# Post-norm transformer block on one core: projections of blocks 3 and 4 moved ahead of and into step 0, roots, doubling and sign activations reordered in the first four steps

## The chip, the cores and the metric
The kernel runs on one core of a Trainium2 chip. The metric is the device time of one execution in microseconds (us); the time of a kernel is the median of its runs.

## The reference
One layer on x of 4096 tokens by 256 channels: sliding-window attention with 16 heads of 16 channels, then a two-layer network with binarised weights, each with a residual and a layer norm behind it.

```python
q = _l2norm(proj(Wq)); k = _l2norm(proj(Wk)); v = proj(Wv)
attn = einsum('bhqd,bhkd->bhqk', q, k)
mask = (rel < 0) | (rel >= 128)              # rel = key position - query position
attn = softmax(attn + where(mask, -1e30, -|rel| * slope_h))
x = layernorm(x + einsum(attn, v) @ Wo.T)
h = gelu(x @ (alpha1 * sign(w1)).T + b1)     # alpha = mean |w| of a row
x = layernorm(x + h @ (alpha2 * sign(w2)).T + b2)
```

## The kernel before
The 4096 tokens are 32 blocks of 128. Each engine has its program written out by hand; the engines meet at semaphores, and each runs its own instructions strictly in the written order. Blocks are projected three steps ahead of their use, so "step i" handles different blocks at a time:

- TensorE (`step` in the tensor program): scores of block i in four chunks of four heads (L342), the query and key projection of block i+3 in two halves between them (`project_qk`, L368), values of block i+1 (`project_v`, L379), the turns of the strips and rows of block i-2 and the output projection (L387, L394, L402), and four chunks of weighted sums (L357). A chunk of scores uses one of two pairs of banks, so chunk 2 waits for the exponential of chunk 0.
- ScalarE: the copy of the weighted sums into strips (L593), four exponentials (`exps`, L616), the copy oT (L599), squares of block i+3 (L569), its root as logarithm and exponential (`norm_of`, L574, L576), and the high halves of block i+2 in float16 (`high_halves`, L583, L586).
- VectorE: `double` of block i+1 (L813, a float16 copy), `outputs` (reciprocal L786, otok L789), the faded values vdiag and vnext (L837, L839), layer norm statistics, the sums of squares and the seed of block i+3 (L859, L769), three operations of a Newton round (`rsqrt_round`, L774, L776, L778), and the normalised block qkn (L876).
- GpSimd: the triangular cuts of each chunk of probabilities (L1162), then the low halves of block i+2 (`low_halves`, L1173, L1175). `double` waits for these.
- SP (the DMA queue): loads of blocks (L243, L244), weights, and `turn_parts` (L256), which transposes the doubled halves into qkT. The scores of a block wait for its transpose. The transpose of block n waits for `double(n)`.

Around the loops stand some extras: dummy matmuls (`keep_warm`, WARM_AGAIN of them ahead of step 0), sign activations of w2 and w1 (`signs2`, `signs1`, L641, L645), and sums of |w2| in halves (`abs_w2`, L908). Steps -3 to -1 prepare blocks 0 to 2; steps 0 to 3 are written out, steps 4 and on are loops. Step 0 has neither queries of a next block nor weighted sums, so it uses chunks of 128x512 instead of 128x1024. After step 31 come eight groups of the two-layer network.

Names of semaphores that the words below use: qkn_done counts normalised blocks, exp_done exponentials, lo_done low halves, parts_ready doubled blocks, otok_done and onorm_done the turned and the scaled outputs, sgn_ready the sign activations.

Of the kernel before, what the change touches and what calls it, by code (L numbers as in the profile page):

```python
# [11 lines left out]
ALU = mybir.AluOpType  # L12
# [3 lines left out]
P = 128  # L16
D = 256
DC = D // P
# [26 lines left out]

WARM_AGAIN = 14

# [54 lines left out]
def norm_base(i, next3):  # L102

    return (i + 3) * NORM_OPS if next3 else NB * NORM_OPS + (i - NB + 3) * (NORM_OPS - 1) - 1
# [7 lines left out]
def build(nc, x, xT, wqkvT, woT, w1, w1T, b1c, w2T, b2, out):  # L112
    with ExitStack() as ctx:
# [215 lines left out]
        def _(pe):  # L329
# [43 lines left out]
            def project_v(i, slot, prev3):  # L373

                count(pe, v_ready, i + 1)
                if prev3:
                    pe.wait_ge(resid_done, i - 2)
                for k in range(DC):
                    mm = nc.tensor.matmul(ps[:, VO, 0:D], xt[:, slot, k, :], wqkv[:, k, 2 * D:3 * D],  # L379
                                          start=(k == 0), stop=(k == DC - 1))  # L380
                mm.then_inc(v_done, 1)
# [63 lines left out]
            pe.wait_ge(wv_in, 16)  # L445
            project_v(-1, 0, False)
            keep_warm(WARM_AGAIN)
            pe.wait_ge(id_made, 2)
            pe.wait_ge(consts, 2)
            step(0, 0, 0, pv=False, prev2=False, prev3=False, both=False)  # L450
            step(1, 1, 1, prev2=False, prev3=False)
            pe.wait_ge(wo_in, 16)
# [45 lines left out]
            def first_hidden():  # L498

                pe.wait_ge(sgn_ready, 2)  # L500
                pe.wait_ge(prep, 1)
                hidden(0, 0, 0)
# [61 lines left out]
        def _(act):  # L564
# [36 lines left out]

            def step(i, par, prev2=True, next2=True, next3=True, prev3=True, early2=False, both=True):
                if prev2:
# [16 lines left out]
                if early2:  # L620
                    high_halves(i, par)
                if prev2:
                    take_rows(i)
                exps(2)
                if next3:
                    squares(i, par)
                exps(3)
                if next3 or prev3:
                    norm_of(i, next3, prev3)
# [8 lines left out]

            def signs2():
                act.wait_ge(w2_in, 16)  # L640
                nc.scalar.activation(sgn2[:], w2_t[:], ACT.Sign).then_inc(sgn_ready, 1)  # L641

            def signs1():
                act.wait_ge(mlp_in, 16 * 3)
                nc.scalar.activation(sgn1[:], w1_t[:], ACT.Sign).then_inc(sgn_ready, 1)  # L645

# [10 lines left out]
            norm_of(-1, True, False)  # L657
            signs2()
            step(0, 0, prev2=False, prev3=False, early2=True, both=False)
            step(1, 1, prev2=False, prev3=False)  # L660
            signs1()
            step(2, 0, prev3=False)
            step(3, 1)
            with act.Fori(0, (NB - 12) // 2) as t:
# [101 lines left out]
        def _(dve):  # L766
# [49 lines left out]
            def split_keys(n):  # L816
# [6 lines left out]
                double(n, n)  # L823

            def step(i, par, cur=True, prev2=True, next1=True, next3=True, prev3=True, prev4=True, aside=None, amid=None):
                base, cols = norm_base(i, next3), norm_columns(next3, prev3)
                norm = (half[:, cols], nt_a[:, cols], nt_b[:, cols], rnorm[:, cols], newton, base)
                if next1:
# [26 lines left out]
                if next3:  # L855

                    dve.wait_ge(sq_done, i + 4)
                    count(dve, newton, base - NORM_OPS + 1)
                    nc.vector.tensor_reduce(ss[:], sq[:].rearrange("p (h d) -> p h d", d=HD), AX.X,  # L859
                                            ALU.add).then_inc(ss_done, 1)  # L860
                    dve.wait_ge(ss_done, i + 4)
                    count(dve, qkn_done, i + 3)
                    if prev3:
                        dve.wait_ge(ln_seed, i - 2)
                    rsqrt_seed(ss[:], half[:, 0:2 * H], (NORM_EPS / QK_SCALE) ** 2, ALU.max, newton)
                if prev2:
# [3 lines left out]
                if next3 or prev3:  # L870
                    rsqrt_round(*norm)
                if next3:

                    dve.wait_ge(newton, base + NORM_OPS)
                    count(dve, lo_done, i + 2)
                    nc.vector.tensor_tensor(qkn[:, 1 - par, :].rearrange("p (h d) -> p h d", d=HD),  # L876
                                            ps[:, QK[1 - par], :].rearrange("p (h d) -> p h d", d=HD),
                                            rnorm[:, 0:2 * H].unsqueeze(2).to_broadcast([P, 2 * H, HD]),
                                            ALU.mult).then_inc(qkn_done, 1)
            nc.vector.memset(mean_ones[:], 1.0 / HID).then_inc(layout, 1)  # L880
# [46 lines left out]
            dve.wait_ge(first_low, 2)  # L927
            step(0, 0, prev2=False, next1=False, prev3=False, prev4=False, aside=lambda: abs_w2(0))
            step(1, 1, prev2=False, prev3=False, prev4=False)
            step(2, 0, prev3=False, prev4=False, aside=lambda: abs_w2(1))  # L930
# [358 lines left out]
```

## Time and profile before
| | us |
|---|---|
| median of 3 runs | 399.65 |
| lowest, highest | 398.71, 401.49 |
| profiled execution, its own time | 399.07 |
| its span, first to last instruction | 397.3 |
| busy TensorE / VectorE / ScalarE / GpSimd | 370.4 / 312.2 / 310.9 / 274.9 |
| mean granted TensorE clock | 0.993 |

The span leaves out 1.8 us of the execution. Busy shares are means over stages with different limits: 30 us of start, attention steps until about 280 us, the network after it. All times below count from the start of the span.

### The profile page before, as it was taken

To read this page: it belongs to the slowest core of one execution; us is meant where nothing else is said; L and a number is where in the kernel's file an instruction comes from. 1 tells how busy PE (TensorE), PEld (TensorE's weight loads), DVE (VectorE), ACT (ScalarE), POOL (GpSimd) and SP (SyncE) were. 2 spreads that over 40 slices of the span, in tenths; PEclk is the share of its full clock that TensorE was granted. 3 is DMA by queue.
4 is the path that set the end of the run, shared out by engine and by line. 5 is a ranking of instruction groups with operands and counts; after the bars stand their busy time and mean duration, and the time that the engine had idled before them with its cause. 6 is when DMAs were issued, how large, how long until landed. Compare 5 with 4: busy or idle time off the path is not lost. (4 is left out here: it accounts for less than half of the span.)

```text
span 397.3 us, 12038 instructions
## 1 busy us (share of the span) xinstructions
PE 370.4 (93%) x3921; PEld 234.9 (59%) x3921; DVE 312.2 (79%) x856; ACT 310.9 (78%) x532; POOL 274.9 (69%) x418
## 2 busy tenths in 40 slices
PE   7788999999999999999999899899999999999991
PEld 5545566655665666556655556555566666666671
DVE  3968777787777777877778878656889998999985
ACT  3688788788877887888788778778988888887744
POOL 1287888888888888888888789888236645655221
PEclk9999999999999999999999999999999999999997
DMA  6694577446434543464345446440022215303112
GB/s 220 143 282 85 120 121 182 86 89 123 106 79 89 121 107 79 88 122 107 79 88 113 94 105 90 89 93 2 1 54 54 79 29 107 106 0 106 55 53 106
DMA packets 98542, 38.28 MB, mean 96 GB/s; under 512 B 84688, under 2 KB 97360, under 8 KB 98256
## 3 DMA queue, kind: packets, MB, share of 16 engines
q1 hardware_dynamic: 98512, 37.89, 43.1%
q8 instruction: 17, 0.28, 0.3%
q14 instruction: 13, 0.11, 0.1%
HBM read 12.72 MB, written 4.19 MB: 43 GB/s over the span
## 5 line engine op out<-in xcount | busy, mean ns | idle before, releaser
L1162 POOL TENSOR_SCALAR_AFFINE_SELECT prob<-prob 128x512 f32<-128x512 f32 x252 | 154.1, 642 | 35.3 <-ACT prob L616 35.3
L616 ACT ACTIVATE prob<-ps 128x1024 f32<-128x1024 f32 (+1 forms) x128 | 125.7, 1014 | 0.7 <-PE ps L342 0.7
L368 PE MATMUL ps<-wqkv,xt 128*128 128x512 f32 x128 | 66.2, 605 | 2.2 <-DVE qkn L876 1.9
L520 PE MATMUL ps<-sgn,prob 128*128 128x256 f16 x512 | 61.5, 273 | 1.5 <-DVE prob L985 1.5
L494 PE MATMUL ps<-yT,sgn 128*128 128x512 f16 x256 | 61.2, 379 | 1.1 <-issue 0.6
L678 ACT ACTIVATE ps<-ps,bias,alpha 128x512 f32<-128x512 f32 x64 | 47.7, 750 | 15.7 <-PE ps L494 12.4
L520 PEld LDWEIGHTS ps<-sgn,prob 128*128 128x128 f16 x512 | 50.0, 98 | 14.8 <-DVE prob L985 2.9
L1221 POOL TENSOR_TENSOR resid<-z,resid 128x256 f32 (+1 forms) x31 | 22.5, 726 | 50.2 <-DVE z L995 50.2
L357 PE MATMUL ps<-prob,vdiag 128*17 128x128 f32 x1024 | 51.2, 274 | 1.7 <-POOL prob L1162 1.6
L342 PEld LDWEIGHTS ps<-qkT 64*128 64x128 f16 x512 | 17.2, 94 | 56.4 <-issue 31.4
L357 PE MATMUL ps<-prob,vnext 128*17 128x128 f32 x992 | 49.7, 273 | 0.0
L342 PE MATMUL ps<-qkT 64*128 64x256 f16 (+1 forms) x512 | 44.2, 272 | 3.2 <-DMA qkT<-parts 2.3
L985 DVE SCALAR_TENSOR_TENSOR prob<-ps,h_scale,prob 128x512 f16<-128x512 f32 x64 | 45.1, 743 | 0.4 <-ACT prob L684 0.3
L593 ACT ACTIVATE strips<-ps 128x512 f32<-128x512 f32 x32 | 19.1, 596 | 27.2 <-PE ps L357 27.2
L859 DVE TENSOR_REDUCE ss<-sq 128x32 f32<-128x512 f32 x32 | 22.0, 686 | 23.1 <-ACT sq L569 22.9
L494 PEld LDWEIGHTS ps<-yT,sgn 128*128 128x128 f16 x256 | 24.6, 98 | 24.4 <-issue 1.0
L684 ACT ACTIVATE prob<-ps,h_scale 128x512 f16<-128x512 f32 x61 | 38.6, 683 | 0.1
L379 PE MATMUL ps<-wqkv,xt 128*128 128x256 f32 x128 | 36.1, 405 | 0.0
L1175 POOL TENSOR_TENSOR parts<-qkn,parts 128x512 f16<-128x512 f32 x30 | 34.8, 1159 | 0.0
L357 PEld LDWEIGHTS ps<-prob,vdiag 128*17 128x17 f32 x1024 | 25.4, 97 | 13.7 <-issue 10.4
L402 PE MATMUL ps<-wo,oT 128*128 128x256 f32 x128 | 33.0, 380 | 0.1
L357 PEld LDWEIGHTS ps<-prob,vnext 128*17 128x17 f32 x992 | 28.1, 98 | 0.0
(105 smaller groups left out, 577.2 us busy)
## 6 DMA issues: line engine op xcount, KB each, us to landing
xt<-in_xT SPq DMA_DIRECT2D x32, 128.0 KB, 2.8
resid<-in_x SPq DMA_DIRECT2D x32, 128.0 KB, 2.3
out_dram<-resid SPq DMA_DIRECT2D x7, 512.0 KB, 2.9
w_t<-in_w2T SPq DMA_DIRECT2D x1, 1024.0 KB, 7.8
w_t<-in_w1T SPq DMA_DIRECT2D x1, 1024.0 KB, 5.0
w_nat<-in_w SPq DMA_DIRECT2D x4, 256.0 KB, 4.2
wqkv<-in_wqkvT SPq DMA_DIRECT2D x3, 256.0 KB, 4.1
qkT<-parts SPq DMA_TRANSPOSE x32, 4.3
```

Of the source, the lines that this page charges most:

```text
L342: mm = nc.tensor.matmul(ps[:, SC + 2 * (c % 2) + hp, 2 * P * t:2 * P * t + wide], qkT[row, here, H // 2 + 2 * c + t, :], queries, start=Tr ...
L357: mm = nc.tensor.matmul(ps[32 * m:32 * m + HD + 1, OT, P * c:P * c + P], v, prob[:, s, CH * c + m, P * (1 - par):P * (1 - par) + P], start ...
L368: mm = nc.tensor.matmul(ps[:, QK[1 - par], :], xt[:, slot, k, :], wqkv[:, k, 0:2 * D], start=(k == 0), stop=(k == DC - 1))
L379: mm = nc.tensor.matmul(ps[:, VO, 0:D], xt[:, slot, k, :], wqkv[:, k, 2 * D:3 * D], start=(k == 0), stop=(k == DC - 1))
L494: mm = nc.tensor.matmul(ps[:, bank, :], sgn1[:, c, P * k:P * k + P], yT[:, par, a, c, :, :], start=(m == 0), stop=(m == 2 * DC - 1))
L520: mm = nc.tensor.matmul(ps[:, banks[b], 0:D], hid[:, par, a, k, P * b:P * b + P], sgn2[:, k, :], start=(m == 0), stop=(m == 2 * HC - 1))
L616: nc.scalar.activation(to, scored, ACT.Exp, scale=QK_SCALE ** -2).then_inc(exp_done, 1)
L678: nc.scalar.activation(bank, bank, ACT.Gelu, bias=bias1[:, k:k + 1], scale=alpha1[:, k:k + 1]).then_inc(gelu_done, 1)
L684: nc.scalar.activation(hid[:, par, 0, k, :], ps[:, hidden_bank(n, k, par), :], ACT.Copy, scale=h_scale[:]).then_inc(hhi_done, 1)
L985: nc.vector.scalar_tensor_tensor(out=hid[:, par, 1, k, :], in0=bank, scalar=h_scale[:], in1=hid[:, par, 0, k, :], op0=ALU.mult, op1=ALU.su ...
L1162: sel = nc.gpsimd.affine_select(out=at, in_=at, compare_op=ALU.is_ge, fill=0.0, base=-near, pattern=[[0, CH], [1 if near else -1, P]], cha ...
L1175: nc.gpsimd.tensor_tensor(parts[:, par, H:2 * H, 2:4, :], src[:, H:2 * H, :].unsqueeze(2).to_broadcast([P, H, 2, HD]), parts[:, par, H:2 * ...
```

## The change
TensorE: block 3's projection (i = 0) goes ahead of step 0, in front of the dummy matmuls, of which 6 are left from 14; block 4's projection stands whole in step 0, behind its first two chunks of scores. Steps 0 and 1 have no projections between their scores any more. ScalarE: squares of block 3 come before step 0, its root stands behind the second exponential of step 0, block 4's squares behind the fourth, and block 4's root behind the second exponential of step 1. The sign activations are in halves: w2's first half ahead of step 0, its second behind step 1, and w1's halves behind the fourth exponentials of steps 2 and 3. VectorE: sums of block 3 ahead of `abs_w2(0)`, its round and normalisation behind it, then `double(2)` and the sums of block 4, all ahead of step 1's values. The later wait for sgn_ready counts 4 instead of 2. GpSimd and SP keep their order.

```diff
-WARM_AGAIN = 14
+WARM_AGAIN = 6
...
             project_v(-1, 0, False)
+            for k in range(DC):
+                project_qk(0, 0, 3, k)
             keep_warm(WARM_AGAIN)
...
+            def project_fourth():
+                for k in range(DC):
+                    project_qk(1, 1, 0, k)
-            step(0, 0, 0, pv=False, prev2=False, prev3=False, both=False)
-            step(1, 1, 1, prev2=False, prev3=False)
+            step(0, 0, 0, pv=False, prev2=False, prev3=False, next3=False, both=False, between=project_fourth)
+            step(1, 1, 1, prev2=False, prev3=False, next3=False)
...
                 exps(1)
                 if early2:
                     high_halves(i, par)
+                if amid:
+                    amid()
...
                 exps(3)
+                if aside:
+                    aside()
...
-            signs2()
-            step(0, 0, prev2=False, prev3=False, early2=True, both=False)
-            step(1, 1, prev2=False, prev3=False)
-            signs1()
-            step(2, 0, prev3=False)
-            step(3, 1)
+            squares(0, 0)
+            signs2(0)
+            step(0, 0, prev2=False, next3=False, prev3=False, early2=True, both=False, amid=lambda: norm_of(0, True, False),
+                 aside=lambda: squares(1, 1))
+            step(1, 1, prev2=False, next3=False, prev3=False, amid=lambda: norm_of(1, True, False))
+            signs2(1)
+            step(2, 0, prev3=False, aside=lambda: signs1(0))
+            step(3, 1, aside=lambda: signs1(1))
...
-            step(0, 0, prev2=False, next1=False, prev3=False, prev4=False, aside=lambda: abs_w2(0))
-            step(1, 1, prev2=False, prev3=False, prev4=False)
+            step(0, 0, prev2=False, next1=False, next3=False, prev3=False, prev4=False)
+            norm_sums(0, False)
+            abs_w2(0)
+            rsqrt_round(*norm_tiles(0, True, False))
+            normalise_rows(0, 0)
+            double(2, 0)
+            norm_sums(1, False)
+            step(1, 1, prev2=False, next1=False, next3=False, prev3=False, prev4=False)
+            rsqrt_round(*norm_tiles(1, True, False))
+            normalise_rows(1, 1)
```

`norm_sums`, `norm_tiles` and `normalise_rows` are the parts of VectorE's step that were written inside it: the sum of squares with the seed, the tiles of the round, and the normalised block.

ScalarE in steps 0 and 1 before: sq are squares, lnx and rnorm the root, prob the exponentials (128x4x128 in step 0), parts the high halves.

```order
L616 ACTIVATE prob<-ps 128x4x128
L569 ACTIVATE sq<-ps 128x512
L616 ACTIVATE prob<-ps 128x4x128
L574 ACTIVATE lnx<-half 128x32
L576 ACTIVATE rnorm<-lnx 128x32
L616 ACTIVATE prob<-ps 128x1024 x3
L569 ACTIVATE sq<-ps 128x512
L616 ACTIVATE prob<-ps 128x1024
L574 ACTIVATE lnx<-half 128x32
L576 ACTIVATE rnorm<-lnx 128x32
```

The same stretch after the change.

```order
L582 ACTIVATE lnx<-half 128x32
L584 ACTIVATE rnorm<-lnx 128x32
L624 ACTIVATE prob<-ps 128x4x128 x2
L577 ACTIVATE sq<-ps 128x512
L624 ACTIVATE prob<-ps 128x1024 x2
L582 ACTIVATE lnx<-half 128x32
L584 ACTIVATE rnorm<-lnx 128x32
L624 ACTIVATE prob<-ps 128x1024 x2
```

Block 3's root has left the place between the steps, and block 4's stands between the second and third exponential of step 1.

VectorE between the values of step 0 and those of step 1 before: w_sum is `abs_w2(0)`, parts the doubling of block 2.

```order
L908 TENSOR_REDUCE w_sum<-w_t 128x128
L859 TENSOR_REDUCE ss<-sq 128x32
L769 TENSOR_SCALAR half<-ss 128x32
L774 TENSOR_TENSOR nt_a<-half,rnorm 128x32
L776 TENSOR_TENSOR nt_b<-nt_a,rnorm 128x32
L778 SCALAR_TENSOR_TENSOR rnorm<-nt_b,rnorm 128x32
L876 TENSOR_TENSOR qkn<-ps,rnorm 128x512
L813 COPY parts<-parts 128x16x32
L837 TENSOR_TENSOR vdiag<-ps,fade 128x16x16
```

The same stretch after the change.

```order
L854 TENSOR_REDUCE ss<-sq 128x32
L789 TENSOR_SCALAR half<-ss 128x32
L939 TENSOR_REDUCE w_sum<-w_t 128x128
L794 TENSOR_TENSOR nt_a<-half,rnorm 128x32
L796 TENSOR_TENSOR nt_b<-nt_a,rnorm 128x32
L798 SCALAR_TENSOR_TENSOR rnorm<-nt_b,rnorm 128x32
L866 TENSOR_TENSOR qkn<-ps,rnorm 128x512
L833 COPY parts<-parts 128x16x32
L854 TENSOR_REDUCE ss<-sq 128x32
L789 TENSOR_SCALAR half<-ss 128x32
L882 TENSOR_TENSOR vdiag<-ps,fade 128x16x16
```

The sums of block 3 are ahead of `abs_w2(0)`, and the sums of block 4 ahead of step 1's values.

ScalarE in step 2 after the change, from the third exponential to the high halves (before, the sign row was not there and all 2048 columns stood ahead of step 2's strips).

```order
L624 ACTIVATE prob<-ps 128x1024
L577 ACTIVATE sq<-ps 128x512
L624 ACTIVATE prob<-ps 128x1024
L656 ACTIVATE sgn<-w_t 128x1024
L582 ACTIVATE lnx<-half 128x32
L584 ACTIVATE rnorm<-lnx 128x32
L591 ACTIVATE parts<-qkn 128x16x16
L594 ACTIVATE parts<-qkn 128x16x32
```

A half of the signs has come in ahead of the root.

## Rows read from the trace of the kernel before

**Rows 1.** Timeline of step 3, then step 25's strips: start, duration, engine, line [idle before]
```profile
38.54 0.60 ACT L593 ACTIVATE strips<-ps 128x512 f32<-128x512 f32 x1 [0.94 <-PE ps L357]
...
40.64 0.39 PE L342 MATMUL ps<-qkT 64*128 64x256 f16 x4
...
40.96 0.44 PE L394 MATMUL ps<-id,otok 128*128 128x128 f32 x2
...
213.36 0.60 ACT L593 ACTIVATE strips<-ps 128x512 f32<-128x512 f32 x1 [0.45 <-PE ps L357]
```

**Rows 2.** Timeline from the end of step 1 into step 2
```profile
28.61 1.90 ACT L645 ACTIVATE sgn<-w_t 128x2048 f16<-128x2048 f32 x1
...
29.07 0.41 PE L357 MATMUL ps<-prob,vdiag 128*17 128x128 f32 x8 [0.54 <-POOL prob L1162]
...
30.41 0.58 ACT L593 ACTIVATE strips<-ps 128x512 f32<-128x512 f32 x1
...
30.73 0.61 PE L342 MATMUL ps<-qkT 64*128 64x256 f16 x8 [1.03 <-DMA qkT<-parts]
...
31.17 1.94 ACT L616 ACTIVATE prob<-ps 128x1024 f32<-128x1024 f32 x2 [0.18 <-PE ps L342]
```

**Rows 3.** Timeline from the projections through steps 0 and 1
```profile
10.98 1.96 PE L368 MATMUL ps<-wqkv,xt 128*128 128x512 f32 x4 [1.92 <-DVE qkn L876]
...
13.46 0.69 DVE L876 TENSOR_TENSOR qkn<-ps,rnorm 128x512 f32<-128x512 f32 x1
...
15.79 0.43 SPq L244 DMA_DIRECT2D resid<-in_x  x1
...
18.04 1.94 DVE L908 TENSOR_REDUCE w_sum<-w_t 128x128 f32<-128x1024 f32 x1
...
20.89 1.15 POOL L1175 TENSOR_TENSOR parts<-qkn,parts 128x512 f16<-128x512 f32 x1
...
21.28 0.69 DVE L859 TENSOR_REDUCE ss<-sq 128x32 f32<-128x512 f32 x1 [1.30 <-ACT sq L569]
...
23.10 2.83 ACT L616 ACTIVATE prob<-ps 128x1024 f32<-128x1024 f32 x3
...
24.51 0.50 DVE L813 COPY parts<-parts 128x512 f16<-128x512 f16 x1
...
27.91 0.57 DVE L774 TENSOR_TENSOR nt_a<-half,rnorm 128x32 f32<-128x32 f32 x1 [0.56 <-ACT rnorm L576]
```

**Rows 4.** DMA issues of 14 to 20 us, then of 24 to 28; last: us to landing
```profile
resid<-in_x SPq DMA_DIRECT2D x1, 128.0 KB, 2.8
...
qkT<-parts SPq DMA_TRANSPOSE x1, 5.4
```

**Rows 5.** Timeline from step 2 into step 3
```profile
36.99 0.61 ACT L586 ACTIVATE parts<-qkn 128x512 f16<-128x512 f32 x1
...
38.38 1.16 POOL L1175 TENSOR_TENSOR parts<-qkn,parts 128x512 f16<-128x512 f32 x1
...
39.61 0.28 DVE L813 COPY parts<-parts 128x512 f16<-128x512 f16 x1
...
40.19 2.40 POOL L1162 TENSOR_SCALAR_AFFINE_SELECT prob<-prob 128x512 f32<-128x512 f32 x4 [0.65 <-ACT prob L616]
```

**Rows 6.** Timeline of a late step, around its doubling
```profile
214.52 0.67 POOL L1203 TENSOR_TENSOR yparts<-resid,yparts 128x256 f16<-128x256 f32 x1
214.59 0.75 DVE L813 COPY parts<-parts 128x512 f16<-128x512 f16 x1 [0.96 <-POOL parts L1175]
...
216.02 0.44 PE L394 MATMUL ps<-id,otok 128*128 128x128 f32 x2 [0.18 <-DVE otok L789]
```

**Rows 7.** Stretches: busy us of PE, PEld, DVE, ACT, POOL; PEclk; DMA share, GB/s
```profile
27.00:30.00 3.00, 2.16 (x64) 1.41 (x64) 2.31 (x6) 2.92 (x6) 3.00 (x6) 1.00 1.24 156
...
388.00:391.90 3.90, 0.96 (x9) 0.61 (x7) 3.32 (x15) 2.71 (x8) 1.34 (x2) 1.00 0.36 129
391.90:397.30 5.40, 0.00 (x0) 0.00 (x0) 1.73 (x8) 1.28 (x4) 0.00 (x0) 0.50 0.29 101
```

More of the change, by code:

```diff
@@ L498, in first_hidden @@
             def first_hidden():
-                pe.wait_ge(sgn_ready, 2)
+                pe.wait_ge(sgn_ready, 4)
                 pe.wait_ge(prep, 1)
@@ L600, in take_rows, with step @@
                                      ACT.Copy).then_inc(ot_ready, 1)
-            def step(i, par, prev2=True, next2=True, next3=True, prev3=True, early2=False, both=True):
+            def step(i, par, prev2=True, next2=True, next3=True, prev3=True, early2=False, both=True, amid=None, aside=None):
                 if prev2:
@@ L637, in norm_of, with signs, signs2, signs1 @@
                 root(half[:, cols], lnx[:, cols], rnorm[:, cols], newton, base, 1)
[L639 to L645, printed above, removed]
+            def signs(dst, src, loaded, times, part):
+                half_ = slice(part * HID, part * HID + HID)
+                flat = "p k n -> p (k n)"
+                act.wait_ge(loaded, 16 * times)
+                nc.scalar.activation(dst[:].rearrange(flat)[:, half_], src[:].rearrange(flat)[:, half_],
+                                     ACT.Sign).then_inc(sgn_ready, 1)
+            def signs2(part):
+                signs(sgn2, w2_t, w2_in, 1, part)
+            def signs1(part):
+                signs(sgn1, w1_t, mlp_in, 3, part)
             nc.scalar.preload_act_table_set("natural_log_exp_and_others")
@@ L823, in split_keys, with norm_tiles, norm_sums, normalise_rows @@
                 double(n, n)
+            def norm_tiles(i, next3, prev3):
+                cols = norm_columns(next3, prev3)
+                return half[:, cols], nt_a[:, cols], nt_b[:, cols], rnorm[:, cols], newton, norm_base(i, next3)
+            def norm_sums(i, prev3):
+                dve.wait_ge(sq_done, i + 4)
+                count(dve, newton, norm_base(i, True) - NORM_OPS + 1)
+                nc.vector.tensor_reduce(ss[:], sq[:].rearrange("p (h d) -> p h d", d=HD), AX.X,
+                                        ALU.add).then_inc(ss_done, 1)
+                dve.wait_ge(ss_done, i + 4)
+                count(dve, qkn_done, i + 3)
+                if prev3:
+                    dve.wait_ge(ln_seed, i - 2)
+                rsqrt_seed(ss[:], half[:, 0:2 * H], (NORM_EPS / QK_SCALE) ** 2, ALU.max, newton)
+            def normalise_rows(i, par):
+                dve.wait_ge(newton, norm_base(i, True) + NORM_OPS)
+                count(dve, lo_done, i + 2)
+                nc.vector.tensor_tensor(qkn[:, 1 - par, :].rearrange("p (h d) -> p h d", d=HD),
+                                        ps[:, QK[1 - par], :].rearrange("p (h d) -> p h d", d=HD),
+                                        rnorm[:, 0:2 * H].unsqueeze(2).to_broadcast([P, 2 * H, HD]),
+                                        ALU.mult).then_inc(qkn_done, 1)
             def step(i, par, cur=True, prev2=True, next1=True, next3=True, prev3=True, prev4=True, aside=None, amid=None):
-                base, cols = norm_base(i, next3), norm_columns(next3, prev3)
-                norm = (half[:, cols], nt_a[:, cols], nt_b[:, cols], rnorm[:, cols], newton, base)
+                base = norm_base(i, next3)
                 if next1:
@@ L855, in step @@
                 if next3:
[L857 to L865, printed above, removed]
+                    norm_sums(i, prev3)
                 if prev2:
@@ L870, in step @@
                 if next3 or prev3:
-                    rsqrt_round(*norm)
+                    rsqrt_round(*norm_tiles(i, next3, prev3))
                 if next3:
[L874 to L879, printed above, removed]
+                    normalise_rows(i, par)
             nc.vector.memset(mean_ones[:], 1.0 / HID).then_inc(layout, 1)
```

## Prediction

> **What bounds the kernel now.** The kernel is a pipeline of 32 attention steps, and I read first what one step hands to the next. ScalarE's strip copy (L593) starts at 38.54 in step 3 and at 213.36 us, 22 steps later [rows 1]: a period of 7.95 us. In one period the chain is: strips, exponential of chunk 0, then TensorE's third scores at 40.64, the turn of the rows at 40.96, and from there TensorE without a gap until the last weighted sum, which releases the next strips [rows 1]. There is no slack in that chain after the strips. So whatever delays or advances the strips and first exponential of step 2 is kept for the rest of the run, and so is every stall put into one step. The change touches only steps -1 to 3, so its worth is one sum of such shifts.
>
> The entry into step 2 is where the timeline shows gaps [rows 2]: the last weighted sum of step 1 starts at 29.07, when GpSimd's last cut allows it; the strips start at 30.41, held by the whole sign activation of 1.90 us at 28.61; the scores of step 2 start at 30.73, when the transposed block 2 has landed, and its first exponential at 31.17. The transpose was issued when block 2 had been doubled, at 25.0 [rows 3], and landed 5.4 us later [rows 4]. Three things are nearly level there: the transpose (30.5), ScalarE's signs (30.4), and GpSimd's cuts (29.0), behind which the last sums run for some 0.65 us.
>
> **Steps 0 and 1 after the change**, in the clock of this trace.
> TensorE: block 3's projection fits where the dummy matmuls were. It needs the second normalised block (L876, 13.46 + 0.69), takes 1.96 us like the projection at 10.98 [rows 3], and is over at 16.2; six dummies follow. The scores of step 0 wait for the same transpose as before. Then `project_fourth` waits for block 4, whose second load is issued at 15.79 and lands 2.8 us later, 18.6 [rows 3, 4]. With 1.96 us for it the third scores come at 20.6, the first scores of step 1 at 22.1 and ScalarE's first wide exponential, 0.44 later as in step 2 [rows 2], at 22.5. Before it was 23.10 [rows 3]. So far the change wins 0.6 us, since ScalarE no longer waits for block 3's root between the steps.
>
> VectorE: block 3's sums (0.69 us and a seed of 0.2) go ahead of abs_w2, which starts about 18.95 instead of 18.04 and takes 1.94 us [rows 3]. The root's round then starts at 20.9. That is the bad moment: GpSimd's long subtraction L1175 starts at 20.89 and runs 1.15 us to 22.04 [rows 3], then come two cuts of 0.6 (four take 2.4 [rows 5]). The trace shows that a small VectorE operation beside a busy GpSimd lasts until GpSimd's current instruction ends: nt_a at 27.91 takes 0.57 us, the copy of double at 24.51 takes 0.50 against 0.28 at 39.61 [rows 3, 5]. So the three operations of the round end at about 22.1, 22.7 and 23.3 instead of taking 0.65 in all; the normalised block 3 is there at 24.0 and block 2 is doubled at 24.4, against 25.0 now. Uncontended it would be 22.8. I take the contended value, as the rows overlap by position, and keep 22.8 for the range.
>
> The Trainium skill, SBUF — State Buffer, "SBUF: two separate sides", says that VectorE and GpSimd share a port pair under an exclusive lock, held for the whole instruction, for VectorE operations with two SBUF inputs or in a two-port mode. Its rule gives the same 24.4, whereas a view in which the engines only share bandwidth would give 22.8; the rows just named side with the lock.
>
> Block 4's sums follow: 0.69 us, and the seed is caught by a cut again, so half is ready at 25.5. ScalarE now has the root of block 4 between its second and third exponential; the second ends at 22.5 + 1.94 = 24.45, so ScalarE waits about 1.05 us for VectorE and starts the third exponential only at 25.95. Two exponentials end at 27.9. The 0.6 won is lost here. GpSimd's last two cuts (1.2 us) start at 28.3 and end at 29.5 instead of 29.0; the last sums start at 29.55, 0.48 later than in [rows 2]. ScalarE's splitting of block 3 and half a sign end at 29.6, the strips start at 30.25 when the sums end, and the first exponential of step 2 at 30.75. The transpose, issued at 24.5, lands by 29.9 if it takes 5.4 again: not last any more.
> Entry: 31.17 - 30.75 = **0.4 us won**. Bounds: with the uncontended value ScalarE does not wait, cuts end at 28.45, the strips come at 29.15 and the exponential at 29.65, 1.5 us won (if the transpose lands in under 5.4); if the transpose still lands at 30.5, 0.2 us won.
>
> **Signs in halves.** Before, all of w1's signs stood in the gap of [rows 2]. Half of them (1024 columns) takes between 0.95, half of 1.90, and 1.04, a 1024-column exponential; I take 1.03. One half now stands in step 2 and one in step 3, between the fourth exponential and the root. ScalarE has 0.94 us idle ahead of the strips at 38.54 [rows 1], so the strips there are hardly later. But the root and the split of the block (L583, L586 until 37.60 [rows 5]) move back by 0.8 us, to 38.4. GpSimd's low halves follow: L1175, now 38.38 to 39.54, ends at 40.3. Now there is a free stretch on GpSimd until the first cut at 40.19 in which VectorE doubles at 39.61 [rows 5]. It is gone: the first cut starts as L1175 ends, and the double, which waits for L1175, meets a busy GpSimd. That case is in the trace: at 214.52 a GpSimd subtraction starts right behind L1175, the double at 214.59 takes 0.75 us, and the turn of the rows starts at 216.02, released by otok, 0.68 us after the double's end [rows 6]. Here the double would run 40.35 to 41.1 and the turn of the rows start at 41.8 instead of 40.96: **0.8 us lost in step 3**. Behind the double are the reciprocal and otok, and TensorE and ScalarE's oT wait for them. Were the double to get in first (0.28 us), the loss is 0.4. The same in step 4 from the second half: 0.8, or 0.4.
>
> **No cost:** eight dummy matmuls fewer, hidden in the wait for block 0's transpose. The half sign ahead of step 0 ends at 17.8, before the first scores are done. SP's order is unchanged; the transpose of block 3 goes out at about 31.7, behind GpSimd's low halves, and has landed by 37.1 even at 5.4 us, ahead of the scores that come just before the strips at 38.54.
>
> **Sum:** -0.4 + 0.8 + 0.8 = **+1.2 us**. The profiled execution took 399.07 us (span 397.3 and 1.8 around it), so 400.3 on its scale; on the median of the three runs, 399.65, it is 400.85. I put the forecast between, at 400.6.
>
> **Rivals.**
> A, the port is free at block 3's root: the entry wins 1.5, stalls cost 1.6: +0.1 us, 399.2 to 399.8. For it: a few tenths in when L1175 runs decide. Against: abs_w2 ends within 0.1 us of its start.
> B, the signs cost nothing: ScalarE's idle 0.94 covers them and the turn of the rows, which could start at 40.57 (39.61 + 0.28 + 0.68 [rows 5, 6]) and starts at 40.96, hides 0.4 more. Then only the entry counts: -0.4 to -1.5, 398.1 to 399.3. Against it are [rows 5, 6].
> C, the early doubling gives nothing, since block 2's transpose is behind w1 and six blocks of loads in the DMA queues; it lands at 30.5 and the entry wins 0.2: +1.4, or 400.8; with more wait at block 4's root up to +2, 401.6.
> D, clearly slower: TensorE's clock falls. The granted clock is 1.00 (2.4 GHz) in all of step 1 with TensorE busy 2.16 of 3 us; at the end of the run it is 0.50 (1.2 GHz) from 391.9, after TensorE had been busy 0.96 of 3.9 us [rows 7]. Fewer dummies and waits in step 1 make TensorE idler. It decides if an idle stretch comes near the 2.9 us that it had before 391.9; I work out 1.5 us at most. One step at the lower clock would add up to the 5.7 us from the third scores to the next strips: 405 us or more.
> The Trainium skill, TensorE: Matmul & The Clock Gate, "What's actually happening", says the throttled state is the default and activity releases it; by that rule D is possible.
>
> **Chances.** Forecast 0.45, A 0.2, B 0.17, C 0.15, D 0.03. A measurement of this kernel tells about 1% (4 us) from no change; the three runs alone span 2.8 us. All but D lie within 1%: same 0.95, faster 0.02 (B with more won on the transpose than I can find), slower 0.03. The range takes the bounds -1.5 to +2 around the two scales: 398.2 to 401.9 us.
>
> **What would show it.** In the profile after: the first wide exponential near 22.5, a gap of about 1 us on ScalarE before block 4's root, nt_a of block 3 over 1 us, double of block 2 near 24.4, its transpose landing before 30, the strips of step 2 near 30.25; double in steps 3 and 4 at 0.75 us and TensorE waiting for otok there; periods of 8.7 us twice, 7.95 after. Strips at 38.1 and 46.1 would mean B. Wrong altogether would be another period than 7.95 in the loop.

## The result and the profile after

The changed kernel takes 401.87 us (median of 20 runs, 400.92 to 403.52) against 400.03 us before (20 runs beside it, 398.71 to 402.11): ratio 1.004, 95% interval 1.0028 to 1.0052, that is 1.1 to 2.1 us slower. The forecast was 1.2 us slower and 400.6 us, inside a range of 398.2 to 401.9. The profiled execution took 401.66 us, its span 399.6. All ratios below leave aside one execution of the experiment e6, which took 613.41 us at a mean granted clock of 0.56.

The timeline of the changed kernel from step 0 to the strips of step 2 (start, duration, engine, line, operation, [idle before <- releaser]):

```profile
18.92 1.98 PE L368 MATMUL ps<-wqkv,xt 128*128 128x512 f32 x4 [0.31 <-DMA resid<-in_x]
...
21.21 1.16 POOL L1214 TENSOR_TENSOR parts<-qkn,parts 128x512 f16<-128x512 f32 x1
...
21.71 0.70 DVE L794 TENSOR_TENSOR nt_a<-half,rnorm 128x32 f32<-128x32 f32 x1
...
22.33 1.22 POOL L1201 TENSOR_SCALAR_AFFINE_SELECT prob<-prob 128x512 f32<-128x512 f32 x2
22.45 0.55 DVE L796 TENSOR_TENSOR nt_b<-nt_a,rnorm 128x32 f32<-128x32 f32 x1
22.66 1.94 ACT L624 ACTIVATE prob<-ps 128x1024 f32<-128x1024 f32 x2
23.04 0.55 DVE L798 SCALAR_TENSOR_TENSOR rnorm<-nt_b,rnorm 128x32 f32<-128x32 f32 x1
...
24.23 0.36 DVE L833 COPY parts<-parts 128x512 f16<-128x512 f16 x1
...
25.73 0.23 ACT L582 ACTIVATE lnx<-half 128x32 f32<-128x32 f32 x1 [1.14 <-DVE half L789]
...
29.71 0.41 PE L357 MATMUL ps<-prob,vdiag 128*17 128x128 f32 x8 [0.54 <-POOL prob L1201]
...
30.41 0.60 ACT L601 ACTIVATE strips<-ps 128x512 f32<-128x512 f32 x1 [0.59 <-PE ps L357]
31.38 0.61 PE L342 MATMUL ps<-qkT 64*128 64x256 f16 x8 [1.03 <-DMA qkT<-parts]
...
31.81 1.94 ACT L624 ACTIVATE prob<-ps 128x1024 f32<-128x1024 f32 x2 [0.80 <-PE ps L342]
```

It follows the working of the prediction closely up to the strips. The first wide exponential is at 22.66 (23.10 in [rows 3]), the three operations of block 3's round take 0.70, 0.55 and 0.55 us beside GpSimd, ScalarE waits 1.14 us for block 4's half, the last sums start 0.64 us later than in [rows 2], and the strips at 30.41. Then comes a row that the forecast did not have: the scores of step 2 wait for the transpose of block 2 until 31.38, and ScalarE waits 0.80 us behind them. The first exponential of step 2 is 0.64 us later than in [rows 2] instead of 0.4 earlier.

Half of that 0.64 us was there before step 0 began. In this execution the granted clock was 0.50 from 11.1 to 14.5 us; the projection in that stretch took 3.37 us instead of the 1.96 of [rows 3], and TensorE came to the first scores of step 0 after their transpose had landed:

```profile
10.71 3.37 PE L368 MATMUL ps<-wqkv,xt 128*128 128x512 f32 x4 [1.92 <-DVE qkn L866]
...
18.21 0.40 PE L342 MATMUL ps<-qkT 64*128 64x128 f16 x8
...
18.53 1.08 ACT L624 ACTIVATE prob<-ps 128x512 f32<-128x512 f32 x2
```

In the kernel before they waited for it:

```profile
17.88 0.40 PE L342 MATMUL ps<-qkT 64*128 64x128 f16 x8 [0.96 <-DMA qkT<-parts]
...
18.21 1.08 ACT L616 ACTIVATE prob<-ps 128x512 f32<-128x512 f32 x2 [0.50 <-PE ps L342]
```

So the first exponential of step 0 was 0.32 us late already. Counted from it, the first exponential of step 2 comes after 12.96 us before and 13.28 us after: the entry itself lost 0.32 us.

The transpose had been issued at 24.66, earlier than before. The DMA issues between 24 and 28 us, with the us to landing last, against the 5.4 of [rows 4]:

```profile
qkT<-parts SPq DMA_TRANSPOSE x1, 6.5
```

Step 3 of the changed kernel, in the same timeline form, around the doubling of block 4:

```profile
39.18 0.60 ACT L601 ACTIVATE strips<-ps 128x512 f32<-128x512 f32 x1 [0.16 <-PE ps L357]
...
39.79 1.22 POOL L1214 TENSOR_TENSOR parts<-qkn,parts 128x512 f16<-128x512 f32 x1
...
40.97 2.44 POOL L1201 TENSOR_SCALAR_AFFINE_SELECT prob<-prob 128x512 f32<-128x512 f32 x4
41.04 0.70 DVE L833 COPY parts<-parts 128x512 f16<-128x512 f16 x1 [1.05 <-POOL parts L1214]
...
42.42 0.44 PE L394 MATMUL ps<-id,otok 128*128 128x128 f32 x2 [0.75 <-DVE otok L809]
...
42.90 0.38 ACT L607 ACTIVATE oT<-ps 128x256 f32<-128x256 f32 x1 [1.29 <-PE ps L394]
...
47.99 0.60 ACT L601 ACTIVATE strips<-ps 128x512 f32<-128x512 f32 x1 [0.24 <-PE ps L357]
...
49.72 0.70 DVE L833 COPY parts<-parts 128x512 f16<-128x512 f16 x1 [1.38 <-POOL parts L1214]
```

GpSimd goes from L1214 straight into the cuts at 40.97, the doubling starts 0.07 us later and takes 0.70 instead of the 0.28 of [rows 5], and TensorE waits for otok. The period of step 3, strips to strips, is 8.81 us, where the kernel before has 7.99; that of step 4 is 8.60 against 7.91. From there on both kernels alternate between 7.99 and 7.91, so the three shifts, 0.64 + 0.82 + 0.69 = 2.15 us, are carried to the end of attention: the last strips start at 279.29 instead of 277.19. The spans differ by 2.3 us. Without the 0.32 us from ahead of step 0 the shifts are 1.83 us, and the medians differ by 1.84.

### The profile page after: what moved, and what is told of

The parts are those of the page before. It is cut to its first block and busy times, and to the rows that moved or that the text cites. A ratio compares the mean times of both kernels' runs of the same rounds, so it can differ in the third digit from the quotient of the medians.

```text
span 399.6 us, 12008 instructions
## 1 busy us (share of the span) xinstructions
PE 369.4 (92%) x3905; PEld 233.3 (58%) x3905; DVE 309.7 (77%) x856; ACT 310.7 (78%) x534; POOL 275.0 (69%) x418
## 5 line engine op out<-in xcount | busy, mean ns | idle before, releaser
L1201 POOL TENSOR_SCALAR_AFFINE_SELECT prob<-prob 128x512 f32<-128x512 f32 x252 | 154.3, 643 | 35.3 <-ACT prob L624 35.3
L1260 POOL TENSOR_TENSOR resid<-z,resid 128x256 f32 (+1 forms) x31 | 22.5, 725 | 50.4 <-DVE z L1034 50.4
L502 PEld LDWEIGHTS ps<-yT,sgn 128*128 128x128 f16 x256 | 24.6, 98 | 24.5 <-issue 1.1
L1214 POOL TENSOR_TENSOR parts<-qkn,parts 128x512 f16<-128x512 f32 x30 | 34.9, 1162 | 0.0
L357 PEld LDWEIGHTS ps<-prob,vdiag 128*17 128x17 f32 x1024 | 25.4, 97 | 13.7 <-issue 10.4
L379 PEld LDWEIGHTS ps<-wqkv,xt 128*128 128x128 f32 x128 | 22.1, 192 | 10.6 <-issue 7.2
```

The costliest lines, as they stand in the source:

```text
L357: mm = nc.tensor.matmul(ps[32 * m:32 * m + HD + 1, OT, P * c:P * c + P], v, prob[:, s, CH * c + m, P * (1 - par):P * (1 - par) + P], start ...
L502: mm = nc.tensor.matmul(ps[:, bank, :], sgn1[:, c, P * k:P * k + P], yT[:, par, a, c, :, :], start=(m == 0), stop=(m == 2 * DC - 1))
L1201: sel = nc.gpsimd.affine_select(out=at, in_=at, compare_op=ALU.is_ge, fill=0.0, base=-near, pattern=[[0, CH], [1 if near else -1, P]], cha ...
```

## The experiments

Each experiment was timed in five rounds against the kernel before on the same chip: e1 to e4 together, e5 to e8 together, e9 to e11 together. They have 11 or 12 executions each, e4 has 6. "Landing" is read from the sixteen semaphore increments of the transpose: the last one, and the last but one in brackets. "Packet" is the start of the first 16 KB packet, after the loads at the start, on queue q8, which the profile names "instruction". "Start" is the first exponential of step 0.

| kernel | ratio to before (95%) | start | packet | issue, landing of block 2's transpose | step 2's first exponential |
|---|---|---|---|---|---|
| before | | 18.21 | 25.4 | 25.08, 30.49 (30.48) | 31.17 |
| changed | 1.0040 (1.0028 to 1.0052) | 18.53 | 29.1 | 24.66, 31.13 (29.65) | 31.81 |
| e1 | 1.0016 (0.9993 to 1.0039) | 17.65 | 28.3 | 23.52, 30.32 (28.84) | 31.00 |
| e2 | 1.0024 (1.0011 to 1.0037) | 18.72 | 29.2 | 24.66, 31.26 (29.78) | 32.03 |
| e3 | 0.9976 (0.9962 to 0.9990) | 18.32 | 28.4 | 24.44, 28.98 (28.76) | 30.69 |
| e4 | 1.0063 (1.0039 to 1.0087) | 18.20 | 26.0 | 25.07, 31.13 (31.11) | 31.81 |
| e5 | 1.0012 (0.9993 to 1.0031) | 18.48 | 29.5 | 25.35, 31.52 (30.02) | 32.42 |
| e6 | 0.9978 (0.9964 to 0.9992) | 18.77 | 24.3 | 25.75, 30.01 (29.98) | 30.68 |
| e7 | 0.9985 (0.9971 to 0.9999) | 18.70 | 28.0 | 24.17, 30.13 (28.63) | 32.12 |
| e8 | 1.0045 (1.0026 to 1.0063) | 18.82 | 29.4 | 24.46, 31.43 (29.92) | 32.41 |
| e9 | 0.9972 (0.9961 to 0.9983) | 18.55 | 23.8 | 24.02, 28.47 (28.41) | 30.45 |
| e10 | 1.0006 (0.9990 to 1.0022) | 17.71 | 25.0 | 24.60, 30.12 (30.10) | 30.80 |
| e11 (e3 again) | 0.9964 (0.9948 to 0.9980) | 18.11 | 28.2 | 23.59, 30.16 (28.58) | 30.84 |

The times of the profiles are of one execution each, and the start alone lies anywhere from 17.65 to 18.82 us, in kernels of both kinds, so times of step 2 are to be compared by their distance from it; the ratios are what the verdicts rest on.

### e1: w1's signs ahead of step 2 again
```diff
-            step(2, 0, prev3=False, aside=lambda: signs1(0))
-            step(3, 1, aside=lambda: signs1(1))
+            signs1(0)
+            signs1(1)
+            step(2, 0, prev3=False)
+            step(3, 1)
```


> The changed kernel with both halves of w1's signs back to back ahead of step 2's strips, as the kernel before had them whole. Theory 1 (the halves inside steps 2 and 3 push the doubling into a busy GpSimd): the doublings of blocks 4 and 5 take 0.28 to 0.30 us again, the periods after step 2 are 8.0 and 7.9, and 1.6 us come back; but w2's second half and w1's signs now stand one behind another at the end of step 1, so step 2's strips start near 31.9 and its first exponential near 32.4, 0.6 later than in the changed kernel: about 0.9 us faster than the changed kernel, some 0.7 us slower than the kernel before. Rival (the loss is all in the entry to step 2, halves cost nothing): periods unchanged at 8.8 and 8.6, and 0.6 us slower than the changed kernel.

Measured: doublings of blocks 4 and 5 in 0.28 and 0.30 us, periods of steps 3 and 4 of 7.99 and 7.91, and a ratio of 1.0016, so by the two ratios about 1 us of the loss is gone, as expected, though the two intervals overlap. The rival, unchanged periods, is out. The strips of step 2 came at 30.20, not 31.9: three half signs in a row took 2.94 us from 27.36 and were mostly covered by the wait for the transpose, which again was the last to arrive (scores at 30.57).

### e2: the halves behind the high halves
```diff
-            step(2, 0, prev3=False, aside=lambda: signs1(0))
-            step(3, 1, aside=lambda: signs1(1))
+            step(2, 0, prev3=False)
+            signs1(0)
+            step(3, 1)
+            signs1(1)
```


> The changed kernel with each half of w1's signs behind the high halves of steps 2 and 3 instead of ahead of the root. ScalarE does the same work in the same steps; only the order against the root and the split differs. Theory 1: GpSimd's low halves are on time, doublings of blocks 4 and 5 at 0.28 to 0.30 us, strips of steps 3 and 4 about 0.15 us late (a half of 1.05 to 1.08 us against 0.94 us of idle time), so periods of 8.1 us instead of 8.8 and 8.6: 1.3 us faster than the changed kernel, 0.3 to 0.6 us slower than the kernel before. Rival (halves cost ScalarE time alone): no difference to the changed kernel.

The timeline of e2 in step 3:

```profile
38.38 1.04 ACT L656 ACTIVATE sgn<-w_t 128x1024 f16<-128x1024 f32 x1
39.26 1.16 POOL L1216 TENSOR_TENSOR parts<-qkn,parts 128x512 f16<-128x512 f32 x1
39.41 0.60 ACT L601 ACTIVATE strips<-ps 128x512 f32<-128x512 f32 x1
...
40.49 0.28 DVE L835 COPY parts<-parts 128x512 f16<-128x512 f16 x1
41.05 2.40 POOL L1203 TENSOR_SCALAR_AFFINE_SELECT prob<-prob 128x512 f32<-128x512 f32 x4 [0.64 <-ACT prob L624]
...
41.83 0.44 PE L394 MATMUL ps<-id,otok 128*128 128x128 f32 x2
```

GpSimd is idle again for 0.64 us ahead of the cuts, the doubling fits in, and TensorE does not wait for otok. ScalarE does the same work as in the changed kernel, in the same steps. The periods of steps 3 and 4 are 7.99 and 7.91. So a half sign there is free, and the place ahead of the root alone cost the 0.7 to 0.8 us of each step. Its ratio is 0.16% below the changed kernel's, 0.6 us, with intervals that overlap; the medians differ by 1.8 us (400.09 and 401.87), but were not timed together. The times that settle it are those of e4 and e10 below.

### e4: the same edit alone, on the kernel before
```diff
-            signs1()
-            step(2, 0, prev3=False)
-            step(3, 1)
+            step(2, 0, prev3=False, aside=lambda: signs1(0))
+            step(3, 1, aside=lambda: signs1(1))
```


> The kernel before with one edit: w1's signs in halves behind the fourth exponentials of steps 2 and 3, as the change has them. Theory 1: doublings of blocks 4 and 5 at 0.70 to 0.75 us, TensorE waits for otok, periods 8.7 to 8.8 and 8.6; the entry does not gain, since the transpose of block 2 lands at 30.5 as before: 1.5 us slower than the kernel before. Rival (the entry is what the change loses, not the halves): within 0.3 us of the kernel before.

Here and in e6 and e10, `signs1(part)` does one half of the columns, as in the change, and the later wait for sgn_ready counts 3.

Measured: 1.9 us slower in the medians (401.36 and 399.44), 1.6 to 3.5 us by the ratio. The doublings took 0.70 us twice and the periods were 8.81 and 8.59, the changed kernel's to 0.01 us. This edit alone gives a loss as large as the change's, and 1.5 us of it are the two stalls. The entry was not level, as expected: the transpose of block 2 took 6.1 us instead of 5.4, and the first exponential of step 2 came at 31.81, 0.64 us late, from an equal start. The edit does not explain that.

### e10: the halves behind the high halves, on the kernel before
```diff
-            signs1()
             step(2, 0, prev3=False)
+            signs1(0)
             step(3, 1)
+            signs1(1)
```


> The kernel before with one edit: w1's signs in halves behind the high halves of steps 2 and 3. Theory (halves cost nothing there and the entry is bound by block 2's transpose): transpose lands at 30.5 and step 2's first exponential stays at 31.2; doublings of blocks 4 and 5 at 0.28 to 0.30 us; within 0.5 us of the kernel before. Rival (the whole signs at the end of step 1 held the entry): first exponential at 30.3 to 30.6, 0.6 us or more faster.

Ratio 1.0006: no difference. Against e4 only the place of the halves differs, four instructions later; that takes the ratio from 1.0063 to 1.0006, and the intervals are apart (1.0039 to 1.0087, 0.9990 to 1.0022). The strips of step 2 came at 29.29, 1.1 us earlier than before (0.6 us counted from the start), and nothing followed from it, as the next rows of its timeline show:

```profile
29.29 0.60 ACT L593 ACTIVATE strips<-ps 128x512 f32<-128x512 f32 x1 [1.07 <-PE ps L357]
...
30.37 0.61 PE L342 MATMUL ps<-qkT 64*128 64x256 f16 x8 [1.15 <-DMA qkT<-parts]
30.80 1.94 ACT L616 ACTIVATE prob<-ps 128x1024 f32<-128x1024 f32 x2 [0.92 <-PE ps L342]
```

In the kernel before, too, the scores of step 2 waited for the transpose [rows 2]; the signs were hidden beneath it.

### e3 and e11: w1's loads behind block 2's transpose
e2, and in SP's program:
```diff
-            for dst, src in ((w1_t, w1T), (bias1, b1c), (bias2, b2)):
-                sp.dma_start(dst[:], src).then_inc(mlp_in, 16)
             for n in range(XS):
                 sp.dma_start(resid[:, n, :], x[n]).then_inc(first_resid, 16)
             load_block(XS + 1, 1)
             turn_parts(2, 2)
+            for dst, src in ((w1_t, w1T), (bias1, b1c), (bias2, b2)):
+                sp.dma_start(dst[:], src).then_inc(mlp_in, 16)
```


> As the run with the halves behind the split, and SP issues the loads of w1, b1 and b2 behind block 2's transpose instead of six loads ahead of it. Theory of the entry (block 2's transpose is held by the loads queued ahead of it, and one late DMA engine): the transpose lands within 4.3 to 4.8 us of its issue at about 24.6, by 29.4; then GpSimd's cuts and the strips bound the entry, first exponential of step 2 at 30.7 to 31.0 instead of 31.8: 0.8 to 1.0 us faster than the run before, near or slightly below the kernel before. Rival (the landing is late for a reason that does not hang on the loads): the first exponential stays at 31.8 and the time is that of the run before.

> The changed kernel with signs behind the split and w1's loads behind the transpose, once more, on the chip of the runs beside it. Expected as in its first run: ratio to the kernel before 0.996 to 0.999, step 2's first exponential near 30.7, strips of step 3 near 38.1. A ratio at or over 1 would say that the first run's gain was chance.

Measured: 0.9976 and 0.9964, so faster than the kernel before by 0.4 to 2.1 us, and e3 is 1.4 us below e2, timed beside it, in the medians; their intervals are apart. In e3 the transpose landed 4.5 us after its issue, the scores of step 2 started at 30.06 with no wait for it, and the first exponential at 30.69. The order of the loads is worth this time. The packets of the trace show how: the transpose moves packets of 256 bytes, and the first of them came 2.3 us after the issue in the changed kernel and 2.6 us in e2, just as the loads ahead ran out, but 1.2 us in e3 and e11. The loads are not all of it, though. In e11, the same kernel, the last increment came 6.6 us after the issue, 1.6 us behind the other fifteen, and yet the time was as good as in e3.

### e6: are the moved projections worth anything?
The kernel before with the edits of e10 and e3.

> The kernel before with the two edits that helped: w1's signs in halves behind the high halves of steps 2 and 3, and the loads of w1, b1 and b2 behind block 2's transpose. Projections, roots and sums stand as in the kernel before. Theory (the moved projections and roots are worth nothing, since block 4's root makes ScalarE wait inside step 1): transpose issued at 25.1, landed by 29.5; GpSimd's cuts end at 29.0, the strips start at 29.8 and step 2's first exponential at 30.2 to 30.4, against 30.7 in the run with the projections moved and the same two edits; 0.2 to 0.5 us faster than that run. Rival (the moved projections win time once transpose and signs are out of the way): 0.5 us or more slower than that run.

Ratio 0.9978, median 398.88, against 0.9976 (398.69) of e3 beside other runs of the kernel before; first exponential of step 2 at 30.68 and 30.69. Counted from the start that is 11.91 us in e6 and 12.37 in e3, so in the profiles e6 leads by 0.46 us, as the theory had it; in the times neither this lead nor the rival's lag shows. With transpose and signs out of the way, the moved projections, roots and doubling are worth nothing that can be measured here; the two intervals would hide up to 0.8 us either way.

### e7: the sums of |w2| behind block 4's normalisation
e3, and in VectorE's program:
```diff
             norm_sums(0, False)
-            abs_w2(0)
...
             normalise_rows(1, 1)
+            abs_w2(0)
```


> The run with the signs behind the split and w1 behind the transpose, and in addition VectorE's first half of the sums of |w2| behind block 4's normalisation, where VectorE was idle for 3.8 us. Theory (VectorE's late start of block 3's round and GpSimd's hold on it make ScalarE wait 1.1 us for block 4's sums): block 3's round starts at 20.6 instead of 21.5, block 4's half is ready 0.5 to 0.9 us earlier, ScalarE's wait ahead of block 4's root shrinks by as much, step 2's first exponential at 29.9 to 30.2 instead of 30.7: 0.5 to 0.8 us faster than the run without it. Rival (the entry is bound by block 2's transpose or GpSimd's low halves even then): no difference.

ScalarE's wait ahead of block 4's root fell from 1.14 to 0.52 us, as expected, but the time did not (398.98 against 398.69, ratios 0.9985 and 0.9976). GpSimd's L1216 still caught the round (nt_b took 1.08 us beside it), and in the profiled execution the last increment of the transpose came at 30.13, 1.5 us behind the others, and the granted clock was at its lower level from 25.4 to 32.2 us. The step of the theory is right, the gain that it promised is not measured.

### e5 and e9: dummy matmuls and the instruction packet
e5 is the kernel before with one number changed; e9 is e7 with eight dummies in step 1:
```diff
-WARM_AGAIN = 14
+WARM_AGAIN = 6
```
```diff
+            def keep_busy(times):
+                for n in range(times):
+                    nc.tensor.matmul(ps[:, OT, 0:P], mean_ones[:], mean_ones[:], start=True, stop=True)
...
+                if dummies:
+                    keep_busy(3)
                 scores(i, 2, par, slot, both)
...
                 scores(i, 3, par, slot, both)
+                if dummies:
+                    keep_busy(5)
                 if next1:
                     project_v(i, (slot + 1) % XS, prev3)
```


> The kernel before with one edit: 6 dummy matmuls ahead of step 0 instead of 14. In the runs so far a 16 KB instruction packet came at 25.4 and 26.0 us with the 14 dummies and at 28.3 to 29.2 us without eight of them. Theory (it is TensorE's instruction stream, which shifts with the number of its instructions, and one DMA engine that carries it is late with its part of block 2's transpose): the packet comes later than 26.5 us, and the landing of that transpose moves with it, its last increment up to 1.5 us behind the others; the time is within 1 us of the kernel before, either way. Rival (the dummies only warm the clock or do nothing): packet at 25.4 and landing at 30.5 as before, same time.

> The run with signs behind the split, w1 behind the transpose and the sums of |w2| behind the roots, and in addition eight dummy matmuls in step 1 where TensorE waited (three ahead of its third scores, five ahead of its values, into a bank that is free there). Theory (instruction packet and block 2's transpose): TensorE's instruction stream has its old length by then, the 16 KB packet comes at 24 to 26 us again, ahead of the transpose's data, all sixteen increments of block 2's landing come together by 29.0, and step 2's first exponential at 29.9 to 30.2: 0.5 to 0.8 us faster than the run with the two edits alone. Rival (the packet's time does not follow TensorE's instructions, or the dummies delay the scores): last increment 1.5 us behind the others again, no gain or a loss of some tenths.

Both moved the packet as the theory has it: e5 from 25.4 to 29.5, e9 back from 28.0 to 23.8. With it went the last increment of block 2's transpose: in e5 it came at 31.52, 1.50 us behind the other fifteen; in e9 they came together, the last at 28.47. The transfers of the changed kernel in the half microsecond from 29.0 (queues: packets, MB, share of 16 engines) show the packet beside the end of the transpose's own packets:

```profile
DMA packets 122, 0.04 MB, mean 80 GB/s; under 512 B 121, under 2 KB 121, under 8 KB 121
## 3 DMA queue, kind: packets, MB, share of 16 engines
q1 hardware_dynamic: 121, 0.02, 23.9%
q8 instruction: 1, 0.02, 12.6%
```

The packet took 1.0 us, from 29.10 to 30.10. The trace has no packet of the transpose between 29.15 and 30.09, and then its last two, of 4 bytes each, at 30.09 and 30.10; the late increment came 1.0 us after them. The last two packets stand at the end of the instruction packet in the same way in all seven late cases of the table. In e3 they came at 28.34 and 28.35, and the instruction packet started at 28.35, just behind them.

In time nothing is seen of it. e5 is 0.1% slower, which its interval does not tell from nothing; e9 (398.42) and e11 (398.45), timed together, are level, though e9's entry took 11.90 us from the start and e11's 12.73. The 0.5 to 0.8 us that the theory had promised for e9 did not come.

### e8: the changed kernel again


> The changed kernel itself, once more, on the chip of these runs. If the first profile is typical: step 2's first exponential at 31.8, doublings of blocks 4 and 5 at 0.70 us, periods 8.8, 8.8, 8.6, then 7.95. The dip of the granted clock at 11.1 us lies ahead of the changed code; if it is a matter of chance it need not come again, and the entry is then up to 0.7 us earlier on TensorE, with the transpose of block 2 still last.

Ratio 1.0045 after 1.0040 the first time, with intervals that overlap widely. Doublings of 0.70 us twice, periods of 8.82 and 8.60 in steps 3 and 4. The dip of the clock at 11.1 us was gone and another stood from 31.3 to 34.7 us, behind a wait of TensorE for the transpose of 1.74 us; the period of step 2 was then 10.83 us instead of 8.77, and this execution took 403.25 us against a median of 401.56. Stretches of e8 (busy us, then PEclk, DMA share, GB/s):

```profile
core 0: us, PE busy (x) PEld busy (x) DVE busy (x) ACT busy (x) POOL busy (x), PEclk, DMA share, GB/s
28.00:31.20 3.20, 1.47 (x40) 0.70 (x32) 0.07 (x1) 2.09 (x4) 3.09 (x5) 1.00 0.56 127
31.30:34.60 3.30, 2.83 (x14) 1.76 (x14) 0.80 (x4) 1.94 (x2) 1.03 (x2) 0.50 0.65 122
```

## Why the prediction was right, and where it was not

**Right: the stalls in steps 3 and 4.** The sum had 0.8 and 0.8 us; the profile has 0.82 and 0.69. The chain was the one described: half sign, late high halves, late low halves, GpSimd straight into the cuts, doubling at 0.70 us (0.75 forecast), TensorE waiting for otok. e4 gives the same two periods from that one edit, and e2 and e10 remove them by moving the half sign four instructions further. Rival B is out.

**Right: the inside of steps 0 and 1.** The exponential at 22.66 (22.5), the round of block 3 done at 23.59 (23.3), the doubling of block 2 done at 24.59 (24.4), the wait of ScalarE 1.14 us (1.05), the strips at 30.41 (30.25). These are times of the span; with the 0.32 us from ahead of step 0 taken off, they lie at the forecast or up to 0.2 us ahead of it. The shares within the round differ: abs_w2 started at 19.85 instead of 18.95, so nt_a started at 21.71 instead of 20.9, met less of L1214 and took 0.70 us, not over 1; in e1, e2 and e7 nt_b was the one caught for 1.08 or 1.09 us. The Trainium skill's rule of the shared port (SBUF — State Buffer, "SBUF: two separate sides") agrees with these rows: nt_a ended at 22.41 and L1214 at 22.37, and the other two operations ended at 23.00 and 23.59, each within 0.06 us of the end of one of GpSimd's two cuts (22.94 and 23.55).

**Wrong: "The transpose, issued at 24.5, lands by 29.9 if it takes 5.4 again: not last any more."** It was issued at 24.66, took 6.5 us and was last. The entry lost 0.32 us, counted from the start, instead of winning 0.4. e2, whose code is the same up to there and whose clock had no early stretch, gives the same: 13.31 us against 12.96, 0.35 lost.

The term that failed is the one put at nothing: "eight dummy matmuls fewer" under **No cost**. Fifteen of the sixteen increments had come at 29.65, 5.0 us after the issue, as the forecast had it. But the 16 KB packet had moved from 25.4 to 29.1, into the end of the transfer, and the sixteenth increment came 1.5 us late, at 31.13. Without that, by an estimate from this profile, the transpose would have been there 0.8 us ahead of the strips at 30.41, and they would have bound the entry. e5 and e9 show that the dummies move the packet and the late increment with it.

The second thing is the backlog, which Rival C named, with a win of 0.2 us left. I took the 5.4 us of [rows 4] as a duration that starts at the issue, but part of it hung on the loads queued ahead. It cost less than the packet: counted from the start, the fifteen increments had landed after 11.1 to 11.2 us in the changed kernel, e1, e2 and e8, and after 10.4 to 10.5 in e3 and e11. Together with the packet it made the transpose last.

How the two share the loss in time is open. That the loads cost time is measured (e3 against e2). For the packet the profiles show it and the times don't (e9 against e11), and the changed kernel with nothing but its eight dummies put back was not run.

**The sum** was 1.2 us and the interval is 1.1 to 2.1. Stalls of 1.5 carry it; the wrong sign of the entry is 0.7 us in the profile. That the forecast is near has some luck in it: the absolute time of 401.87 lies at the very top of the range, and the top doesn't follow from the bounds that it names (399.65 + 2 is 401.65, not 401.9). I had also written that a measurement tells about 1% from no change; with 20 runs on each side the interval was 0.12% to either side. The size of the entry's loss is less sure in the medians: e10 puts sign halves without the moved projections at 1.0006, e2 with them at 1.0024, 0.7 us more, with intervals that touch.

**Rival D, the clock,** did not decide the median, but I set it aside too easily. Both profiles of the changed kernel have a stretch at half clock, one ahead of the changed code, one in step 2, the latter after TensorE had been busy 1.47 of 3.2 us, with less idle time in one piece than the 2.9 us that I took as the mark. The first made step 0 start 0.46 us later behind its transpose (0.92 us from landing to first exponential, against 0.46 before) and left its execution at the median (401.66 and 401.87 us); with the second, the execution took 1.7 us over its median, not the 5.7 us that I worked out.

**Left open.** Whether fewer dummies make such stretches of the clock more frequent was not tried by itself, but the mean granted clock of nearly every execution is on record. It is 0.990 or less in 61 of 103 executions of kernels with six dummies and in 23 of 133 with fourteen in all; in e5, where nothing else was changed, in 5 of 12 against 4 of 34 of the kernel before beside it. The means do not tell where the stretches stood. Executions more than 1.2 us over the median of their runs are no more frequent with six (14 of 103) than with fourteen (20 of 153). Whose instructions the packet holds is inferred from e5 and e9, which differ in TensorE's program alone from the kernel before and from e7; no row names the engine. Why the transpose took 5.4 us in the kernel before and 6.1 in e4, with all increments together and the packet at 25.4 and 26.0, was not tried.

## What to carry to other kernels

In a pipeline without slack a helper instruction of 1 us is not placed by the idle time of its own engine alone: the same half sign cost 0.7 to 0.8 us ahead of a root and nothing behind that root and two more copies, because two engines further on a copy lost its gap in GpSimd's work. When a transfer is the last to arrive, look at what is queued ahead of it before making its data ready sooner; here the early data won nothing that could be measured and the order of the loads won 0.3 to 0.5% (e6 against e10, e3 against e2). And see whether the last increment comes with the others or alone: in the first case the transfer is slow, in the second something held one part of it.

## What the runs showed of the hardware

One 16 KB instruction packet on queue q8 took 1.0 us, and in seven of eight profiles in which it came at 28.0 to 29.5 us, at the end of the transpose's own packets, one of the sixteen increments of that transpose came 1.5 to 1.6 us behind the others. In the eighth, e3, the packet started at 28.35, as the transpose's last packets had just gone, and the last increment was 0.2 us behind. For block 3's transpose there is one case each way: in e6, with a packet at 35.3, the last increment was 1.4 us behind (35.88 and 37.32); in e9, with a packet at 35.3 too, it was not (35.88 and 35.94). The number of dummy matmuls ahead moves the packet: it came at 23.8 to 26.0 us in the five profiles with fourteen in all and at 28.0 to 29.5 in the eight with six. A transpose of 0.5 MB landed 4.3 us after its issue where no load stood ahead of it (block 3's in the kernel before, the changed kernel and e1, e2, e8); with 0.6 to 0.7 MB of loads still on their way at its issue it took 5.4 to 6.1 us with all increments together (block 2's in before, e10, e4). And the granted clock of TensorE (1.00 or 0.50, that is 2.4 or 1.2 GHz) had stretches at the lower level at differing places in executions of one and the same kernel: 11.1 to 14.5 us and 31.3 to 34.7 us in the changed kernel, 10.9 to 14.3 us in e3 and 26.5 to 29.9 us in e11.
